# Exponentials of turned scores read from PSUM, in an attention kernel on one core

## The reference, cut to what matters

```python
# block L0: self attention, cross attention to ctx_2048, then an MLP
scores = einsum('bhqd,bhkd->bhqk', q, k) / sqrt(16)
scores = scores * mask - 10000.0 * (1.0 - mask)
probs = softmax(scores, axis=-1)
ctx = einsum('bhqk,bhkd->bhqd', probs, v)
x = x + mlp(layernorm(x + ctx @ w_o + b_o))            # gelu, tanh form
# block L1: latents = x attend to concat([ctx_2048, latents]), then an MLP
attn = einsum('bkhd,bnhd->bhkn', q, kmat) / 16
attn = softmax(where(full_mask, attn, -inf), axis=-1)
out = mlp(rmsnorm(attn @ v @ out_w + out_b + residual))  # gelu
return out + residual
```

## Time and profile before

| | us |
|---|---|
| median of 3 executions | 1120.99 |
| lowest, highest | 1120.76, 1122.2 |
| span of the profiled execution, first to last instruction | 1120.9 |
| TensorE busy in it | 1077.3 |
| VectorE busy | 973.0 |
| ScalarE busy | 960.3 |
| GpSimd busy | 560.8 |

### The profile page before, as it was taken

The page is one execution under the profiler, slowest core; times in us unless marked ns, Lnnn a source line. Parts: engine busy times, 40 slices in busy tenths (PEclk is TensorE's granted clock), DMA queues, the critical chain, the costliest instruction groups (busy, mean ns, idle before and its releaser), DMA issues.

```text
span 1120.9 us, 46846 instructions
## 1 busy us (share of the span) xinstructions
PE 1077.3 (96%) x19624; PEld 942.0 (84%) x19624; DVE 973.0 (87%) x2360; ACT 960.3 (86%) x2155; POOL 560.8 (50%) x807
## 2 busy tenths in 40 slices
PE   6688999999999999999999999999999999999998
PEld 5677788888888888888888888888888888888887
DVE  4899988888899888889988888999888899998774
ACT  3558988998888899988888998888899888899887
POOL 3757555454544545454454445455444555554322
PEclk9999999999999999999999999999999999999999
DMA  7541000000000000000000000000000000000000
GB/s 262 185 163 40 17 19 15 9 15 19 14 13 19 20 15 18 19 14 13 19 19 20 14 18 19 8 19 19 19 15 19 19 8 20 23 8 8 7 7 21
DMA packets 30435, 34.13 MB, mean 30 GB/s; under 512 B 11920, under 2 KB 28048, under 8 KB 29200
## 3 DMA queue, kind: packets, MB, share of 16 engines
q1 hardware_dynamic: 30224, 31.14, 8.7%
HBM read 26.93 MB, written 4.19 MB: 28 GB/s over the span
## 4 chain that ended last, share of the span: by engine, by line
PE 57%; DVE 24%; ACT 7%; POOL 6%; issue 4%; DMA 1%; SPq 0%; DVEq 0%; ACTq 0%; POOLq 0%
PE psum L482 23%; PE psum L662 11%; PE psum L622 6%; PE psum L495 5%; PE psum L456 4%; PE psum L589 3%; PE psum L608 3%; DVE mx_self L1318 3%; POOL prob_self L2561 3%; DVE prob_self L1337 3%; DVE late L1301 3%; DVE prob_self L1308 2%; DVE spread_lat L1268 2%; DVE mx_ctx L1318 2%; ACT xn_mlp L1967 1%
## 5 line engine op out<-in xcount | busy, mean ns | idle before, releaser
L2561 POOL TENSOR_TENSOR prob_self<-prob_self,add_self 128x512 f32<-128x512 f32 x64 | 84.8, 1342 | 146.8 <-DVE prob_self L1308 146.7
L2561 POOL TENSOR_TENSOR prob_cross<-prob_cross,add_cross 128x512 f32<-128x512 f32 x64 | 81.0, 1286 | 88.8 <-DVE prob_cross L1308 88.8
L2040 ACT ACTIVATE staging<-psum,cols,undo_in 128x128 f32<-128x128 f32 x256 | 95.8, 456 | 2.2 <-PE psum L482 1.7
L2040 ACT ACTIVATE hid_mlp<-psum,folded,undo_in 128x128 f32<-128x128 f32 x256 | 97.0, 472 | 0.1
L662 PE MATMUL psum<-hi_m,parts_mlp 128*128 128x256 f16 x512 | 94.6, 273 | 0.9 <-DVE parts_mlp L1370 0.9
L662 PE MATMUL psum<-hi_n,staging 128*128 128x256 f16 x512 | 94.1, 273 | 1.1 <-ACT headsT_lat L1988 0.6
L482 PE MATMUL psum<-xT_mlp,hi_m 128*128 128x128 f16 x1024 | 92.6, 219 | 0.1
L482 PE MATMUL psum<-xT_mlp,hi_n 128*128 128x128 f16 x1024 | 92.5, 219 | 0.0
L2567 POOL TENSOR_TENSOR late<-late,mx_ctx 128x512 f32<-128x512 f32 x64 | 67.2, 1050 | 45.2 <-DVE mx_ctx L1324 42.1
L482 PE MATMUL psum<-xT_mlp,lo_n 128*128 128x128 f16 x512 | 89.0, 219 | 0.0
L482 PE MATMUL psum<-xT_mlp,lo_m 128*128 128x128 f16 x512 | 89.0, 219 | 0.0
(11 more groups left out here) (281 smaller groups left out, 4045.8 us busy)
## 6 DMA issues: line engine op xcount, KB each, us to landing
xin<-in_x SPq DMA_DIRECT2D x32, 128.0 KB, 2.1
ctxT<-in_ctxT SPq DMA_DIRECT2D x32, 128.0 KB, 2.0
late<-in_ctxT SPq DMA_DIRECT2D x4, 1024.0 KB, 9.0
late<-in_x SPq DMA_DIRECT2D x4, 1024.0 KB, 6.6
out<-xb SPq DMA_DIRECT2D x32, 128.0 KB, 2.1
staging<-in_w_m SPq DMA_DIRECT2D x2, 1024.0 KB, 6.6
staging<-in_w_n SPq DMA_DIRECT2D x2, 1024.0 KB, 5.4
mask<-in_mask_cross SPq DMA_DIRECT2D x32, 32.0 KB, 1.9
```

What stands on the lines that cost most here:

```text
L2040: last = e.activation(hid[t][g][:, j * P:(j + 1) * P], ps[:, j * P:(j + 1) * P], ACT.Gelu_apprx_tanh, bias=b1[:, 4 * g + j:4 * g + j + 1], ...
L2561: e.tensor_tensor(ch, ch, over_heads(a[:, :]), ALU.add).then_inc(sem["added_" + t], 1)
```

## The change

The transposition is moved ahead of the exponential. TensorE turns the shifted scores, and the exponential reads them from PSUM and writes the tile `probT`; the in-place exponentials and the copies are gone. The signals exp_self, exp_cross, exp_ctx and exp_lat are gone with them. In ScalarE's order each `exponential(u, t, a)` now stands where `prob_out(u, t, a)` stood, and the old calls of `exponential` are removed. Every other call of ScalarE, the orders of all other engines, and all banks are as before.

```diff
             @of_unit
             def prob_turn(u, t, b):
 
-                q.wait_ge("exp_" + t, 2 * u + 2)
+                q.wait_ge("shifted_" + t, 2 * u + 2)
                 claim(b, ("prob_turn", t, 1, u), "probT_" + t, 2 * u + 2)
...
             @of_unit
-            def exponential(u, t, h):
-                q.wait_ge("shifted_" + t, 2 * u + h + 1)
-                e.activation(prob[t][h][:, :], prob[t][h][:, :], ACT.Exp).then_inc(sem["exp_" + t], 1)
-
-            @of_unit
-            def prob_out(u, t, a):
+            def exponential(u, t, a):
                 src = bank[in_bank["prob_turn", t, a, u]][:, :].rearrange("p (n t) -> p n t", n=NP)
                 q.wait_ge("prob_turn_" + t, u + 1)
                 q.wait_ge("mix_" + ("lat" if t == "ctx" else t), u)
-                e.copy(probT[t][a][:, :, :], src).then_inc(sem["probT_" + t], 1)
+                e.activation(probT[t][a][:, :, :], src, ACT.Exp).then_inc(sem["probT_" + t], 1)
```

ScalarE's order in a slot, in full:

```diff
             for t in range(FILL, SLOTS):
-                exponential(t - 5, "ctx", 0)
-                exponential(t - 5, "lat", 0)
-                exponential(t - 5, "ctx", 1)
                 heads_out(t - 3, "self")
-                exponential(t - 5, "lat", 1)
                 gelu(t - 7, "mlp1", 0)
                 gelu(t - 4, "mlp0", 0)
                 normalize(t - 3, "cross")
                 hidden_hi(t - 4, "mlp0", 0)
                 high_half(t - 3, "cross")
                 gelu(t - 4, "mlp0", 1)
-                prob_out(t - 5, "lat", 0)
-                prob_out(t - 5, "ctx", 0)
-                prob_out(t - 5, "lat", 1)
+                exponential(t - 5, "lat", 0)
+                exponential(t - 5, "ctx", 0)
+                exponential(t - 5, "lat", 1)
                 hidden_hi(t - 4, "mlp0", 1)
                 normalize(t - 2, "self")
-                prob_out(t - 5, "ctx", 1)
+                exponential(t - 5, "ctx", 1)
                 values(t - 5, "lat")
                 high_half(t - 2, "self")
                 normalize(t - 6, "mlp1")
                 hidden_hi(t - 7, "mlp1", 0)
                 gelu(t - 7, "mlp1", 1)
                 values(t - 2, "self")
                 lat_out(t - 4)
+                high_half(t - 6, "mlp1")
+                values(t - 3, "cross")
                 exponential(t - 3, "cross", 0)
                 exponential(t - 3, "cross", 1)
-                high_half(t - 6, "mlp1")
-                values(t - 3, "cross")
-                prob_out(t - 3, "cross", 0)
-                prob_out(t - 3, "cross", 1)
                 heads_out(t - 5, "lat")
-                exponential(t - 2, "self", 0)
                 hidden_hi(t - 7, "mlp1", 1)
                 heads_out(t - 3, "cross")
+                values(t - 4, "ctx")
+                exponential(t - 2, "self", 0)
                 exponential(t - 2, "self", 1)
-                values(t - 4, "ctx")
-                prob_out(t - 2, "self", 0)
-                prob_out(t - 2, "self", 1)
                 normalize(t - 3, "mlp0")
                 high_half(t - 3, "mlp0")
```

In the start and the tail the same is done. In the first two parts of the tail the exponentials of ctx and lat come in this way to stand between single Gelus, the first part as an example:

```diff
             high_half(UNITS - 3, "cross")
-            prob_out(UNITS - 5, "ctx", 0)
+            exponential(UNITS - 5, "ctx", 0)
             normalize(UNITS - 2, "self")
             gelu(UNITS - 4, "mlp0", 1)
-            prob_out(UNITS - 5, "ctx", 1)
+            exponential(UNITS - 5, "ctx", 1)
             high_half(UNITS - 2, "self")
-            prob_out(UNITS - 5, "lat", 0)
+            exponential(UNITS - 5, "lat", 0)
             hidden_hi(UNITS - 4, "mlp0", 0)
             hidden_hi(UNITS - 4, "mlp0", 1)
             gelu(UNITS - 7, "mlp1", 1)
             normalize(UNITS - 6, "mlp1")
-            prob_out(UNITS - 5, "lat", 1)
+            exponential(UNITS - 5, "lat", 1)
```

More of the change, by code:

```diff
@@ L2063, in _ @@
             exponential(0, "self", 0)
-            exponential(0, "self", 1)
-            prob_out(0, "self", 0)
             high_weight(0, "q")
             values(0, "self")
-            prob_out(0, "self", 1)
+            exponential(0, "self", 1)
             heads_out(0, "self")
@@ L2078, in _ @@
             normalize(3, "self")
+            values(0, "cross")
             exponential(1, "self", 0)
             exponential(1, "self", 1)
-            values(0, "cross")
-            prob_out(1, "self", 0)
-            prob_out(1, "self", 1)
             high_weight(0, "m2")
@@ L2105, in _ @@
             values(3, "self")
+            normalize(0, "mlp0")
+            high_half(0, "mlp0")
             exponential(1, "cross", 0)
-            normalize(0, "mlp0")
+            high_half(4, "self")
             exponential(1, "cross", 1)
[L2109 to L2112, removed]
             normalize(2, "cross")
@@ L2136, in _ @@
             normalize(3, "cross")
-            prob_out(2, "cross", 0)
-            prob_out(2, "cross", 1)
+            exponential(2, "cross", 0)
+            exponential(2, "cross", 1)
             hidden_hi(1, "mlp0", 1)
@@ L2147, in _ @@
             exponential(0, "ctx", 1)
+            exponential(4, "self", 0)
             exponential(4, "self", 1)
[L2149 to L2154, removed]
             lat_out(1)
-            exponential(3, "cross", 0)
-            exponential(3, "cross", 1)
             normalize(2, "mlp0")
@@ L2161, in _ @@
             high_half(2, "mlp0")
-            prob_out(3, "cross", 0)
-            prob_out(3, "cross", 1)
+            exponential(3, "cross", 0)
+            exponential(3, "cross", 1)
             values(1, "lat")
@@ L2169, in _ @@
             hidden_hi(2, "mlp0", 1)
+            heads_out(3, "cross")
+            lat_out(2)
             exponential(1, "ctx", 0)
@@ L2173, in _ @@
             exponential(1, "lat", 1)
[L2174 to L2179, removed]
             normalize(0, "mlp1")
@@ L2269, in _ @@
             high_half(UNITS - 1, "self")
-            exponential(UNITS - 4, "lat", 0)
-            exponential(UNITS - 4, "ctx", 0)
-            exponential(UNITS - 4, "lat", 1)
-            exponential(UNITS - 4, "ctx", 1)
             gelu(UNITS - 3, "mlp0", 0)
@@ L2276, in _ @@
             normalize(UNITS - 2, "cross")
-            prob_out(UNITS - 4, "ctx", 0)
-            prob_out(UNITS - 4, "ctx", 1)
+            exponential(UNITS - 4, "ctx", 0)
+            exponential(UNITS - 4, "ctx", 1)
             high_half(UNITS - 2, "cross")
@@ L2282, in _ @@
             gelu(UNITS - 3, "mlp0", 1)
-            prob_out(UNITS - 4, "lat", 0)
-            prob_out(UNITS - 4, "lat", 1)
+            exponential(UNITS - 4, "lat", 0)
+            exponential(UNITS - 4, "lat", 1)
             values(UNITS - 4, "lat")
@@ L2307, in _ @@
             high_half(UNITS - 2, "mlp0")
-            exponential(UNITS - 3, "lat", 0)
-            exponential(UNITS - 3, "ctx", 0)
-            exponential(UNITS - 3, "lat", 1)
-            exponential(UNITS - 3, "ctx", 1)
             gelu(UNITS - 5, "mlp1", 0)
@@ L2316, in _ @@
             hidden_hi(UNITS - 2, "mlp0", 0)
-            prob_out(UNITS - 3, "ctx", 0)
-            prob_out(UNITS - 3, "ctx", 1)
-            prob_out(UNITS - 3, "lat", 0)
-            prob_out(UNITS - 3, "lat", 1)
+            exponential(UNITS - 3, "ctx", 0)
+            exponential(UNITS - 3, "ctx", 1)
+            exponential(UNITS - 3, "lat", 0)
+            exponential(UNITS - 3, "lat", 1)
             values(UNITS - 3, "lat")
@@ L2326, in _ @@
             values(UNITS - 1, "cross")
+            normalize(UNITS - 4, "mlp1")
+            lat_out(UNITS - 2)
             exponential(UNITS - 1, "cross", 0)
             exponential(UNITS - 1, "cross", 1)
-            normalize(UNITS - 4, "mlp1")
-            lat_out(UNITS - 2)
-            prob_out(UNITS - 1, "cross", 0)
-            prob_out(UNITS - 1, "cross", 1)
             high_half(UNITS - 4, "mlp1")
@@ L2339, in _ @@
             high_half(UNITS - 1, "mlp0")
-            exponential(UNITS - 2, "ctx", 0)
-            exponential(UNITS - 2, "lat", 0)
-            exponential(UNITS - 2, "ctx", 1)
-            exponential(UNITS - 2, "lat", 1)
             gelu(UNITS - 1, "mlp0", 0)
@@ L2347, in _ @@
             hidden_hi(UNITS - 1, "mlp0", 1)
-            prob_out(UNITS - 2, "ctx", 0)
-            prob_out(UNITS - 2, "lat", 0)
-            prob_out(UNITS - 2, "ctx", 1)
+            exponential(UNITS - 2, "ctx", 0)
+            exponential(UNITS - 2, "lat", 0)
+            exponential(UNITS - 2, "ctx", 1)
             normalize(UNITS - 3, "mlp1")
-            prob_out(UNITS - 2, "lat", 1)
+            exponential(UNITS - 2, "lat", 1)
             gelu(UNITS - 4, "mlp1", 0)
```

55 lines of the change are left out of this document (15 added, 40 removed).

## The result

| | before | after |
|---|---|---|
| median of 4 executions, us | 1121.13 | 1203.83 |
| lowest, highest | 1120.76, 1122.2 | 1202.61, 1207.75 |
| profiled execution, first to last instruction | 1120.9 | 1206.0 |

The ratio is 1.0742 with a 95% interval of 1.0729 to 1.0755: slower by 7.4%, or 83 us. The profiled execution of the changed kernel is the one of 1207.75 us, 3.9 above the median, and the traces are compared with that in mind.

What follows compares the result with a forecast made beforehand. TensorE was taken to set the pace in the repeated slots, with late ScalarE results costing time. The sum was 1120.9 + 68 (slots) - 1 (start) + 10.5 (tail) = 1198 us, range 1155 to 1220.

Steps and rivals of the forecast that it cites:

- The bound: In the repeated slots TensorE sets the pace (109.66 of 110 us); work taken from ScalarE buys nothing there by itself.
- The loads: On ScalarE 65 activation table loads become 127, four a slot for two; the 62 added ones take 80 us.
- The slot: One of 25 repeats on ScalarE: 2.73 us more, 35.3 for 32.6; 68 us for all 25.
- The slower read: Exponentials reading PSUM instead of SBUF: 0.05 us more a slot, at the most 0.25.
- The first place: Self attention's x: a load after the Gelu delays it, so TensorE stands still 1.33 us a slot at v_self.
- The sign that was named: TensorE's queue would show new waits of about 1.3 us, 25 times, at v_self (L495) for the low half.
- The second place: Cross mix: a load between the values of cross and the cross exponentials stops TensorE another 1.35 us a slot.
- "one-place" rival: Only one of the two places in a slot costs: about 1159 us; 20 in 100 with the half-way cases.
- ScalarE's busy time: Whole kernel: from 960 us, less 160 for removed work, plus 80 for loads, to about 880 us.
- The start: Ahead of the repeated slots: load count unchanged, exponentials leaving chains save a little; -1 us.
- The tail: After the last slot: 12 added loads in four parts, 4.4 + 4.4 + 1.7 + about 0; +10.5 us, within 0 to 17.
- The price of a switch: Each table change on ScalarE costs the load's 1.28 us and the lost overlap of 0.1, 1.38 us, without a drain.

Runs made afterwards that it cites:

- experiment 1: The changed kernel with the exponential from PSUM replaced by a Copy, so the exponentials are left out; 1119.78 us, ratio 0.9983.
- experiment 7: The kernel before with self and cross turned first behind the start only, plus a one-column exponential behind lat_out; 1121.84 us, ratio 1.0000.
- Experiment 8: The kernel before with only a one-column exponential added ahead of the first copy of lat in each of 25 slots; 1193.86 us, ratio 1.064.
- Experiment 9: The changed kernel with hidden_hi and the self normalization moved ahead of the first three lat and ctx exponentials in the slots; 1262.99 us, ratio 1.126.
- Experiment 6: The changed kernel plus a one-column exponential behind lat_out, bringing the load ahead of the cross exponentials forward; 1184.68 us, ratio 1.0567.
- Experiments 2 and 3: The kernel before with, respectively, only self and cross turned first (1161.43 us, ratio 1.0364) and only ctx and lat turned first (1206.73 us, ratio 1.0762).
- Experiment 4: The kernel before with the turn first only for units whose softmax lies ahead of the repeated slots; 1124.99 us, ratio 1.0034.
- experiment 5: The kernel before with the turn first only for units whose softmax lies behind the repeated slots; 1135.65 us, ratio 1.0128.

## Why the prediction was right, and where it was not

- **The bound.** TensorE at 109.66 of 110 us, and work taken from ScalarE buys next to nothing: shown by experiment 1 (0.17%, with 221 us of ScalarE's work gone) and 7 (none).
- **The loads.** 127 was counted from the order and 127 are in the trace. Experiment 8 shows that 50 added loads alone cost 72 us, and experiment 1 that without the loads nothing is lost.
- **The slot.** 35.3 was forecast, 35.13 measured; 68 us for 25 slots, 63.4 measured. The slower read was priced at 0.05 us; L2021 takes 595 to 600 ns where the copy took 589. The walk on ScalarE came out closely: lat_out was forecast to end 2.75 us late and ends 2.82 late.
- **The first place, right in size, wrong in where TensorE would wait.** 1.33 us was forecast as a wait ahead of v_self, with the banks of the cross scores to "fall into the same 1.33 us and don't add to it". That v_self begins late by this much holds: it is 1.25 late. But the scores stand ahead of v_self in TensorE's queue, so the wait is nearly all there: 1.10 us for the banks, and 0.15 are left for v_self. The sign that was named, 1.3 us 25 times at v_self (L495), is not in the trace. Experiment 9 shows that banks freed 1.1 us later cost 1.12 a slot; the prediction had the banks about 1 us late, as they are.
- **The second place.** 1.35 was forecast; the mix waits 1.01 and the turn before it 0.28 longer than before. Experiment 6 takes back 19 us by moving the load alone; where only self and cross are changed, experiment 7 takes back all. Experiments 2 and 3 together show that the two places are not independent. The forecast walked through the slot in order and so had the whole; its "one-place" rival took 25 x 1.35 = 34 us for either. The cross place alone gave 25 x 1.28 = 32 in the slots, beside the start and the lower clock in some slots (40 us in all), and the other place alone gave 85.
- **ScalarE's busy time.** Forecast about 880, measured 907.8. The step was 256 x 0.625. Two neighbouring exponentials take 1.15 us together, 0.1 less than twice 0.625; durations added up count the overlap twice. It changed nothing in the sum of the time.
- **The start, wrong in sign.** -1 was forecast, "In the start neither count changes". The count is indeed the same, but the place was not asked after: one load moved onto a chain that TensorE waits for, as in the slots. Experiment 4 has about +4; in the traces 1.9 us of it is the moved load and 1.2 to 1.4 the lower clock behind it. With the exponentials taken out, experiment 1 reaches the first slot 0.6 us early, near the -1.
- **The tail, under-sized.** +10.5 was forecast, the trace has 15.8 and experiment 5 has 13.5 by itself. The failing step is the price of each part, 4.4 + 4.4 + 1.7 + 0. The trace has 6.2 and 5.3 us for the first two and 4.3 for the rest, of which 0.1 falls into the last 29 us, so the last part was priced rightly and the third at less than half. In the first two TensorE's clock, taken as full, is 0.91 over 20 us each (1052 to 1072 and 1092 to 1112 us); in the third it is 1.00, so there it is waits. How they share out among the loads was not tried.
- **How much of the hit was luck.** The three terms were off by -4.6 (slots), +6.9 (start) and +5.3 (tail) in the profiled execution, so errors of both signs are in the 1198. By the medians the forecast is 5.8 us short.
- **The price of a switch.** The row's 1.28 us and the lost overlap gave 1198 against 1203.8 measured. The price in the page "ScalarE: Activation LUTs" of the Trainium skill (section "What ACT_TABLE_LOAD costs"), which adds a drain to each load, would have given an estimate of some 139 us for the slots alone, where 63.4 were measured. In variant 7 the load begins 0.03 us behind lat_out and the next activation 0.01 us after its end, and the loads in the slots of the other traces stand as close; no drain is seen. The rule in its section "Rules for kernel authors", to do all of one table set before the next, is borne out: the order that breaks it is 83 us slower.

## What to carry to other kernels

Ahead of moving an exponential, write down ScalarE's order as a string of table sets and count the changes; 256 removed instructions were outweighed by 62 that no line of the source names. Then ask where each load falls, also where the count stays the same. A load does not wait for the data of its activation (in the changed kernel's tail one ends at 1108.87, and its exponentials wait 2.18 us more for TensorE), so a one-column activation put where the engine idles anyway moves the load off the chain. Where another engine sets the pace, price a change of order by the position of each result that this engine waits for, its banks included, and not by busy time.

## What had not been expected of the hardware

TensorE's granted clock fell after stalls in the middle of full work. In the changed kernel's slots its weight loads wait 1.19 us ahead of the cross scores and 1.21 at the mix, and the clock stays at 1.00. In variant 2, with one wait of 1.49 us a slot, every fourth or fifth slot has a stretch near 1.2 GHz and takes 35.0 in place of 33.9 us. In variant 9, with waits of 2.43 and 1.42 us, 18 of 24 slots have such a stretch and take about 37.85 in place of 36.25. In the start the same 32 matmuls took 4.32 or 6.93 us. There, behind the same stall of 1.79 us in the same code, the clock over 120 to 128 us is 1.00 in variant 9 and 0.77 in the changed kernel. Why one stall brings the fall and another of like length doesn't was not settled.
